# A feed-forward network in two passes of seven block products each

## The reference

```python
mod = silu(c) @ W_mod + b_mod
sh_msa, sc_msa, g_msa, sh_mlp, sc_mlp, g_mlp = split(mod, 6)
x = x + g_msa * attention(layernorm(x) * (1 + sc_msa) + sh_msa)
x = x + g_mlp * (gelu((layernorm(x) * (1 + sc_mlp) + sh_mlp) @ W1 + b1) @ W2 + b2)
```

## Time and profile before

| | |
|---|---|
| median of 3 runs | 2998.91 us (2998.82 to 3001.7) |
| the profiled execution's own time | 2999.62 us |
| its span, first to last instruction | 2997.8 us |
| mean granted clock of TensorE | 0.997 of full speed |

### The profile page before, as it was taken

How to read it: one execution, slowest core, us unless ns; L and a number is a source line. 1 busy time by engine, 2 the same in 40 slices (tenths; PEclk the granted TensorE clock), 3 DMA queues, 4 the chain that set the end, 5 groups by cost and what they waited for, 6 DMA issues and landing times.

```text
span 2997.8 us, 63187 instructions
## 1 busy us (share of the span) xinstructions
PE 2961.3 (99%) x25634; PEld 2419.0 (81%) x25634; DVE 1986.8 (66%) x2891; ACT 1390.0 (46%) x2875; POOL 787.1 (26%) x513
## 2 busy tenths in 40 slices
PE   8999999999998999999999999999999999999998
PEld 5999889999886777777777777777888888888887
DVE  4589886565535888888888888887565433343432
ACT  2366654323213777777777777776223211211111
POOL 1011110000001444444444444445553110111110
PEclk9999999999999999999999999999999999999999
DMA  5643326563595333333333333332672010010100
GB/s 184 221 160 112 113 90 249 215 228 99 187 320 172 109 94 86 86 86 93 93 87 93 89 100 90 86 86 78 249 258 92 29 36 1 29 36 29 36 15 15
DMA packets 223352, 339.35 MB, mean 113 GB/s; under 512 B 29096, under 2 KB 142920, under 8 KB 218728
## 3 DMA queue, kind: packets, MB, share of 16 engines
q1 hardware_dynamic: 214212, 329.08, 34.3%
q0 software_dynamic: 576, 6.29, 0.6%
q10 hardware_dynamic: 8292, 0.05, 0.2%
HBM read 211.15 MB, written 124.20 MB: 112 GB/s over the span
## 4 chain that ended last, share of the span: by engine, by line
PE 65%; DMA 1%; DVE 1%; ACT 0%; issue 0%; POOL 0%; SPq 0%; DVEq 0%; ACTq 0%; POOLq 0%
PE b_po L1787 16%; PE b_ps L1758 12%; PE d_pf L2261 12%; PE d_po L2272 12%; PE b_tp_act L1770 7%; PE c_po L2034 3%; PE b_tp_dve L1770 3%; DMA c_ot<-o_t 1%; DVE c_ol L2050 0%; PE d_pt L2253 0%; DVE o_first_rest L2050 0%; ACT b_p L1726 0%; POOL d_y L2202 0%; DVE norm_st L1082 0%; DVE x_second_rest L2057 0%
## 5 line engine op out<-in xcount | busy, mean ns | idle before, releaser
L1817 DVE TENSOR_REDUCE b_nm<-b_ps 128x1 f32<-128x1024 f32 x512 | 602.0, 1217 | 17.8 <-PE b_ps L1758 4.5
L1726 ACT ACTIVATE b_p<-b_ps,b_nm 128x1024 f32<-128x1024 f32 x512 | 564.6, 1112 | 8.9 <-DVE b_nm L1817 8.9
L1787 PE MATMUL b_po<-b_pt,b_v 128*64 128x256 f32 x4096 | 498.4, 385 | 0.8 <-DVE b_pt L1837 0.8
L1731 ACT ACTIVATE b_pt<-b_tp_act 128x512 f32<-128x512 f32 x512 | 307.9, 601 | 305.6 <-PE b_tp_dve L1770 305.6
L1837 DVE COPY b_pt<-b_tp_dve 128x512 f32<-128x512 f32 x512 | 351.4, 686 | 117.6 <-PE b_tp_dve L1770 117.5
L1770 PEld LDWEIGHTS b_tp_act<-ident,b_p 64*128 64x128 f32 x4096 | 311.7, 138 | 116.9 <-issue 100.6
L1787 PEld LDWEIGHTS b_po<-b_pt,b_v 128*64 128x64 f32 x4096 | 272.1, 136 | 128.4 <-ACT b_pt L1731 0.9
L2236 ACT ACTIVATE d_ge<-d_pf,b_t 128x512 f32<-128x512 f32 x128 | 88.2, 689 | 575.6 <-PE d_pf L2261 575.6
L1770 PE MATMUL b_tp_act<-ident,b_p 64*128 64x64 f32 x4096 | 347.6, 225 | 2.4 <-issue 2.4
L1770 PE MATMUL b_tp_dve<-ident,b_p 64*128 64x64 f32 x4096 | 348.2, 225 | 0.0
L2327 DVE CAST d_gh<-d_ge 128x512 fp32r<-128x512 f32 x128 | 64.6, 505 | 404.0 <-ACT d_ge L2236 403.8
(11 more groups left out here) (344 smaller groups left out, 6428.9 us busy)
## 6 DMA issues: line engine op xcount, KB each, us to landing
b_raw_q<-q_t SPq DMA_DIRECT2D x124, 256.0 KB, 4.2
k_t<-p_out SPq DMA_DIRECT2D x64, 256.0 KB, 2.2
q_t<-p_out SPq DMA_DIRECT2D x64, 256.0 KB, 2.3
v_n<-p_out SPq DMA_DIRECT2D x64, 256.0 KB, 3.6
b_v<-v_n SPq DMA_DIRECT2D x32, 512.0 KB, 3.9
b_raw_k<-k_t SPq DMA_DIRECT2D x124, 128.0 KB, 4.3
c_ot<-o_t SPq DMA_DIRECT2D x7, 2048.0 KB, 10.5
a_x<-x SPq DMA_DIRECT2D x32, 256.0 KB, 3.1
```

Of the source, the lines that this page charges most:

```text
L1726: act.activation(pr[k % 4][:], ps[k % 2][:], ACT.Exp, bias=nm[:, k % 4:k % 4 + 1], accum_out=rs[:, n:n + 1]).then_inc(exp_done, 1)
L1731: act.activation(dst, src, ACT.Copy).then_inc(t_out[0], 1)
L1787: mm = pe.matmul(po[rows, (blk % 2) * 2 * P:(blk % 2 + 1) * 2 * P], vt[u][:, kc, rows], pt[blk % 2][h][:, kc, :], start=(kc == 0), stop=(k ...
L1817: dve.tensor_reduce(nm[:, k % 4:k % 4 + 1], ps[k % 2][:], axis=AX.X, op=ALU.max, negate=True).then_inc(max_done, 1)
```

## The change

The feed-forward network becomes two passes, each with seven block products.

- Pass 1 (`hidden`) goes over 32 tiles v = 4g + p: group g of 512 rows and piece p of W1. A tile's seven products (12 matmuls of 256 columns each) land in five banks. ScalarE copies the first, VectorE makes five sums, ScalarE does the Gelu of four blocks in halves of 256 columns, and GpSimd makes four sums of the Gelu blocks, which are the operand sums of pass 2. The seven blocks, 256 KB each, are written to a tensor in HBM, `hidden_blocks`. A tile's seven places in SBUF are one of two sets; a set is free when its stores have landed (`free`). Stores are issued in two parts, `store_kept` (three blocks) and `store_sums` (four).
- Pass 2 (`back`) reads the 224 blocks back one by one through a ring of 14 places, 7 of them ahead. Each is split (`high_r` on ScalarE, `rest_r` on VectorE) and used in 12 matmuls of 256 columns. Seven banks accumulate over the four pieces, and `drained` empties them after each group: three plain sums, then four gated ones, each with a multiplication in place, and GpSimd's four additions.
- Four pieces of W1 are loaded, summed and split: two in `output_projection`, two within pass 1's first group. W2's four pieces take the same places: the first three are loaded as pass 1's last tiles free them, the last at its end. The first seven blocks of pass 2 are loaded and split within pass 1's last group.
- TensorE waits for the operand parts product by product (`NEEDED`), no longer once for a whole operand.
- Row statistics for the second group move into the last group of `output_projection`.

The core of the diff (the loops that set the order; the rest renames places and semaphores):

```diff
...
-    cols = t["w_qkv"].rearrange("(k p) n -> p k n", p=P)
+def load_w(queue, t, o, p, loaded, name="w_qkv"):
+    cols = t[name].rearrange("(k p) n -> p k n", p=P)
...
-                        for n in (2 * g - 2, 2 * g - 1):
-                            sp.dma_start(w1_part(w1_raw, n), w1_part(t["w1"].rearrange("(k p) n -> p k n", p=P), n)).then_inc(w1_in, 16)
+                    if g == 1:
+                        load_w(sp, t, w[0], 0, w1_in, "w1")
                 else:
+                    sp.wait_ge(m_done, g * GT)
+                    sp.wait_ge(w1_in, 32)
+                    load_w(sp, t, w[1], 1, w1_in, "w1")
+                    sp.wait_ge(o_split, g * KO)
+                    sp.wait_ge(y_out[0], 16 * B)
+                    sp.wait_ge(y_out[1], 16)
+                    sp.dma_start(y1[:], y2[512:1024, :].rearrange("(a p) f -> p a f", p=P)).then_inc(y1_in, 16)
                     for n in range(GT):
+                        if n == GT - 1:
+                            sp.wait_ge(m_done, NG * GT)
+                            sp.wait_ge(w1_in, 64)
+                            load_w(sp, t, w[2], 2, w1_in, "w1")
                         sp.wait_ge(y_done, g * GT + n + 1)
                         sp.dma_start(y2[(g * GT + n) * P:(g * GT + n + 1) * P, :], yt[hf][:, n, :]).then_inc(y_out[hf], 16)
+                    sp.wait_ge(w1_in, 96)
+                    load_w(sp, t, w[3], 3, w1_in, "w1")
...
+                if g in (3, NG - 1):
+                    p = g // 4
+                    act.wait_ge(w_sums, 4 * p + 4)
+                    for m in range(4):
+                        act.copy(flat(high(w[p], *GROUPS[m])), flat(raw(w[p], *GROUPS[m]))).then_inc(w_high, 1)
...
+                if r in (11, 28):
+                    p = r // 28
+                    dve.wait_ge(w1_in, 32 * p + 32)
+                    for n in range(4):
+                        block_sum(dve, w[p], SUMS_W, n, w_sums, 4 * p)
...
+                if r in (30, 31):
+                    rest_w(1, 2 * (r - 30))
+                    rest_w(1, 2 * (r - 30) + 1)
...
+    ORDER = (0, 5, 4, 6, 1, 2, 3)
+    RING, LEAD = 14, 7
+    TURNS = (0, 2, 1, 3)
...
+        PRODUCTS = ((0, 0, p_a, True), (5, 5, p_b, True), (4, 3, p_d, True), (6, 4, p_e, True),
+                    (1, 1, p_a, False), (2, 2, p_f, True), (3, 6, p_e, False))
...
+        def free(engine, v, kind):
+            if v >= 2:
+                engine.wait_ge(out_done[v % 2][kind], 32 * (v // 2))
...
+            def store_kept(v):
+                sp.wait_ge(gelu_done, 4 * v + 4)
+                for first, last in ((0, 2), (3, 4)):
+                    sp.dma_start(gq[v][:, first:last, :], places[v % 2][:, first:last, :]).then_inc(out_done[v % 2][0], 16)
...
+                v, i = block_of(n)
+                if n % 28 == 0:
+                    for u in range(2):
+                        for kind in range(2):
+                            sp.wait_ge(out_done[u][kind], 32 * 2 * (n // 28 + 1))
+                if n >= RING:
+                    sp.wait_ge(n_done, n - RING + 1)
+                if n >= 4:
+                    sp.wait_ge(r_in[n % 4], 16 * (n // 4))
+                o, r = ring_place(n)
+                sp.dma_start(flat(raw(o, r)), gq[v][:, i, :]).then_inc(r_in[n % 4], 16)
...
+                if v == NV - NP:
+                    sp.wait_ge(m_done, 7 * (NV - NP))
+                    for n in range(LEAD):
+                        load_block(n)
+                if g == NG - 1:
+                    if p == NP - 1:
+                        sp.wait_ge(m_done, 7 * NV)
+                        for n in range(LEAD, LEAD + 4):
+                            load_block(n)
+                    load_w2(p)
+                store_kept(v)
+                store_sums(v)
+                if v == NV - NP:
+                    sp.wait_ge(z_done, GT * NG)
+                    load_rows(0)
+            for n in range(LEAD + 4, RING):
+                load_block(n)
...
+            for v in range(NV):
+                g, p = divmod(v, NP)
+                if p == 0 and 1 <= g < NG - 1:
+                    rstds(g + 1)
+                u = places[v % 2]
+                for n, (o, a, b, op) in enumerate(SUMS_W):
+                    if n == 0:
+                        pool.wait_ge(gelu_done, 4 * v + 3)
+                    else:
+                        pool.wait_ge(s_sums, 4 * v + n)
+                    if n == 2:
+                        pool.wait_ge(gelu_done, 4 * v + 4)
+                    pool.tensor_tensor(u[:, o, :], u[:, a, :], u[:, b, :], op).then_inc(s_sums, 1)
...
+                    cols = slice(i * 256, (i + 1) * 256)
+                    a = act.activation(places[v % 2][:, place, cols], src[:, cols], ACT.Gelu, bias=b1[:, j + i:j + i + 1])
...
+                act.wait_ge(m_done, 7 * v + 1)
+                free(act, v, 1)
+                act.copy(u[:, 4, :], p_a[:]).then_inc(copies, 1)
+                if v:
+                    act.wait_ge(sums, 5 * v)
+                    gelu(v - 1, 1, places[(v - 1) % 2][:, 1, :])
+                if v == 1:
+                    act.wait_ge(prev.y_done, B * BT)
+                    for m in range(4):
+                        high_w(2, m)
+                if v == 2:
...
+                if more and p == 3:
+                    for m in range(0 if g == 0 else 2, 4):
+                        high_x(g + 1, m)
+                if more and p == 1:
...
+                if v >= NV - 2:
+                    for m in range(4):
+                        high_w(NP + v - NV + 2, m)
+                act.wait_ge(m_done, 7 * v + 5)
+                free(act, v, 0)
+                gelu(v, 0, p_a)
+                act.wait_ge(sums, 5 * v + 3)
+                gelu(v, 3, u[:, 3, :])
+                if more and p == 1:
+                    modulate(g + 1, 2)
+                    modulate(g + 1, 3)
+                if more and p == 2 and g:
+                    high_x(g + 1, 0)
+                    high_x(g + 1, 1)
+                act.wait_ge(sums, 5 * v + 4)
+                gelu(v, 2, u[:, 2, :])
+            act.wait_ge(sums, 5 * NV)
+            gelu(NV - 1, 1, places[(NV - 1) % 2][:, 1, :])
+            for n in range(LEAD, NB + LEAD):
+                if n in (LEAD, LEAD + 8):
+                    for m in range(4):
+                        high_w(NP + 2 + (n - LEAD) // 8, m)
...
+            def bank_free(v, step):
+                if step == 0 and v:
+                    pe.wait_ge(gelu_done, 4 * v - 3)
+                if step == 1 and v:
+                    pe.wait_ge(sums, 5 * v - 4)
+                if step == 2 and v:
+                    pe.wait_ge(sums, 5 * v - 3)
+                if step == 3 and v:
+                    pe.wait_ge(sums, 5 * v)
+                if step == 4:
+                    pe.wait_ge(copies, v + 1)
+                if step == 5 and v:
+                    pe.wait_ge(sums, 5 * v - 1)
+                if step == 6:
+                    pe.wait_ge(sums, 5 * v + 3)
...
+                    pe.wait_ge(x_rest, 4)
+                for step, (wi, xi, out_, start) in enumerate(PRODUCTS):
+                    bank_free(v, step)
+                    if p == 0 and g and step in NEEDED:
+                        pe.wait_ge(x_rest, 4 * g + NEEDED[step])
+                    if g == 0 and step in (0, 1, 3):
+                        pe.wait_ge(w_rest, 4 * p + (1, 3, 3, 4)[step])
+                    if v == 0 and step == 5:
+                        pe.wait_ge(prev.gated_done, B * BT)
+                    hidden(g, p, wi, xi, out_, start)
+                    if g + 1 < NG and p == 1 and step in (1, 2, 4, 5):
+                        transposes(g + 1, (1, 2, 4, 5).index(step))
+            for n in range(NB):
+                v, i = divmod(n, 7)
+                g, p = divmod(v, NP)
+                if g == 0 and i in NEEDED:
+                    pe.wait_ge(w_rest, 4 * (NP + p) + NEEDED[i])
...
+                if g and p == 0:
+                    if i == 0:
+                        pe.wait_ge(d_copies, g)
+                    pe.wait_ge(d_sums, 7 * (g - 1) + (0, 1, 2, 4, 5, 6, 7)[i])
+                pe.wait_ge(r_rest, n + 1)
...
+                        dve.wait_ge(w1_in, 96)
+                        for n in range(3):
+                            w_sum(2, n)
+                    if at_ == (0, 3):
+                        w_sum(2, 3)
+                    if at_ == (0, 4):
+                        dve.wait_ge(w1_in, 128)
+                        for n in range(3):
+                            w_sum(3, n)
+                    if at_ == (1, 0):
+                        w_sum(3, 3)
+                    if at_ == (1, 1):
+                        rest_w(2, 0)
+                    if at_ == (1, 2):
+                        normed(1, 2)
+                        rest_w(2, 1)
+                    if at_ == (1, 3):
+                        normed(1, 3)
+                    if at_ == (1, 4):
+                        rest_w(2, 2)
```

(58 more changed lines are left out.)

668 lines of the change are left out of this document (378 added, 290 removed).

## The result

The changed kernel takes 2982.21 us (2979.05 to 2983.45, 4 runs) against 3000.03 (2998.82 to 3001.7, 4 runs) before: a ratio of 0.9938, 95% interval 0.9925 to 0.995. That is 18 us less where 46 were forecast, and 0.2 us outside the range. Its profiled execution took 2979.05 us, 25 more than the forecast's sum of 2954.0.

What follows compares the result with a forecast made beforehand. TensorE, busy 99% of the span, was taken as the bound. Terms: 2999.62 - 60.6 + 7 + 4 + 4 = 2954.0 us by the profiled execution, 2953 by the median; range 2941 to 2982, chance 0.8.

Steps and rivals of the forecast that it cites:

- first group, stalls: Pass 1's first group: TensorE waits for normalisations while two W1 pieces are still made; +7 us (4 to 11).
- groups 1 to 6, stalls: Pass 1's groups 1 to 6: late third sums and ScalarE's copy waiting for stores; +4 us (0 to 25).
- last group, stalls: Pass 1's last group: no term of its own; DMA called hidden at 1.8 MB of blocks a tile, 175 GB/s.
- handover (pieces 1 to 4): From pass 1 to pass 2: waits for W2's late pieces and ScalarE's casts; +4 us (2 to 7).
- pass 2 afterwards: Rest of pass 2: VectorE's draining falls 3 to 6 us behind, covered by a lead of 8.6 us; 0 us.
- The matmuls: Feed-forward stage: 5376 narrow matmuls for 3072, 119.7 ns each; 657.8 us against 718.4, 60.6 us less.
- the rival of dear narrow matmuls: Feed-forward matmuls of 256 columns at 171 ns instead of 119.7: stage 933 us, kernel 3213 us; chance 0.01.
- One of the prediction's own signs: Pass 1: the prediction is wrong if tiles take above 11 us after the first group.
- The factor 1.4 for VectorE beside GpSimd: Pass 1: block sums and subtractions beside GpSimd cost 1 to 1.8 times their price; 1.4 taken.
- The second rival: VectorE beside GpSimd as second bound: 20 to 40 us instead of 15, 2960 to 2980, at 2972; chance 0.25.
- The places' loop: Pass 1's copy awaits stores from two tiles before: 8.9 us a turn, under 10.5; as bounding rival 3034 us, chance 0.05.
- The end: After the last product: sum, multiplication, GpSimd's last addition and two stores, 7.4 us against 8.1; 0 us with the start.

Runs made afterwards that it cites:

- e6: Changed kernel with GpSimd's four additions of each tile covering 32 of 512 columns, order and waits kept; 25.2 us faster by the medians.
- e16: Changed kernel with GpSimd's additions cut to 32 of 512 columns, each behind a 4-column power that keeps the chain long; 2967.24 us.
- e3: Changed kernel with loads of blocks 0 to 6 ahead of tile 27's stores and the end's first rows loaded in pass 2; last group 3.8 us shorter.
- e14: e12 with VectorE's third and fourth addition of the tile before moved from behind the second to behind the fourth sum; 3026.11 us.
- e12: Changed kernel with e11's move, casts spread, block loads before tile 27's stores, two normalisations earlier, end loads one by one; groups 1 to 6 259.4 us.
- e15: Changed kernel with only the additions of tiles 0 to 30 moved to VectorE, at e14's later places; 3047.55 us.
- e11: Changed kernel with additions of tiles 0 to 30 on VectorE, behind the next tile's first and second sums; groups 1 to 6 from 257.8 to 260.7 us.
- e10: e6 plus four 512-column GpSimd additions per tile on a tile nothing waits for, after the stores are released; 2962.97 us.
- e7: Changed kernel with TensorE waiting for all four operand parts before a group's or piece's first product; 13.3 us slower by the medians.

## Why the prediction was off

Terms up to the last matmul; the bare time is 41.8 us a group with transposes (e6: 250.6/6), and 40.2 a group without or four pieces (336 x 119.7 ns).

```
                                forecast   measured
pass 1, bare                       336.0      332.6
pass 2, bare                       321.8      321.8
first group, stalls                  7.0        9.9
groups 1 to 6, stalls                4.0        7.2
last group, stalls                   0         13.4
handover (pieces 1 to 4)             4.0       11.0
pass 2 afterwards                    0          0.5
sum                                672.8      696.4
```

- **The matmuls** were right: 120 ns, full clock wherever TensorE isn't stopped. This is the whole gain, and the rival of dear narrow matmuls is out. Pass 1's term was 3.4 us too high.
- **The last group** is the step that failed, with 13.4 of the 23.6 us missed. The forecast's sum has no term for it: I called DMA hidden by the 1.8 MB of a tile's blocks alone, and took for its VectorE the load of the steady groups. In each of its last three tiles four W2 operand sums and two or three subtractions of blocks stand beside the five sums, in the last two four subtractions of W2's parts as well. e16 and e6 show 6.6 us for the contention and 3.6 for the chain, which leaves 3.2. e3's 3.8 us for the order on SP lie within these and are not to be added. One of the prediction's own signs came here: tiles above 11 us after the first group (13.4 in the mean; 10.7 in groups 1 to 6).
- **The handover** was mis-sized, 11.0 for 4 (2 to 7). Its mechanism, ScalarE's casts waiting for W2's sums ahead of the blocks' casts, held: spreading them gives 4.0. What I left out is the 2 MB burst at block 20, which shows once that stall is gone, and the clock.
- **First group and groups 1 to 6** were mis-sized by 2.9 and 3.2, inside their ranges. The factor 1.4 for VectorE beside GpSimd was close for subtractions (1608/1219 = 1.32); the normalisations, which I left at their own price, were the ones that doubled, and TensorE waits for just those (8.1 us).
- **The clock** was in no term: 9.0 us, spread over the rows above. Stalls were priced as if only their own length counted.
- **The second rival**, at 2972, named the cause best: e6 puts its price at 25 us, of which the additions' place in the chain is a part. I gave it 0.25. Its sizes were not right: subtractions at 1.32 and not 1.8 times their price, additions at 1.43 us and not 2.28, 7.2 us and not 18 in groups 1 to 6, and it had no term for the last group either. That 2972 lies nearer to the measured time than 2953 is in part luck.
- **The places' loop** was rightly judged near its bound and not on it.
- **The end** took 2.1 us more, not none: a gate multiplication beside GpSimd took 1.26 to 1.36 instead of 0.69 us, three times over. The start gave back 0.8.

The Trainium skill (SBUF — State Buffer, "Who interferes with whom") was used for its rule on two SBUF inputs. What it says of one input holds only outside VectorE's two-port modes, a condition that the prediction left out; it also says that `tensor_scalar` can run in such a mode and then contends. That d_z doubles, while the statistics (679 and 678 ns) and the sums with a PSUM operand (688 and 690) do not change, agrees with it; whether d_z runs in that mode no run here shows.

## What to carry to other kernels

When a stage gets shorter, work out each engine's load again for its first and last group, where extra loads and operand making stand, and not for the steady part alone. A stall of TensorE is priced with what follows it: here 29 us of waits came with 9 us lost at the lower clock. An addition on a "free" engine has two prices, the traffic it puts beside its neighbour and the chain it stands in; before moving it, find both the operation that it would delay and the buffer that it would release later: here the early place took back in one stretch what it gave in others, and the place three products later cost 62 to 67 us (e14 against e12, e15 against e11).

## What the runs showed of the hardware that I had not expected

- GpSimd doubled a VectorE operation with a single SBUF tile as input: d_z took 1020 ns in the mean (up to 1517) beside additions, 541 without them. The trace before had shown it once: of four such normalisations (c_z), the first ran beside a GpSimd addition and took 1516 ns, the others 534.

```profile
L2084 DVE TENSOR_SCALAR c_z<-c_y,norm_mv,norm_rstd x4: 534/534/1516, 2135.0 to 2137.3; 128x512 f32<-128x512 f32 x4
```

- It is not GpSimd being busy that does it: powers of 4 columns, 1.02 us each and as much GpSimd time, left VectorE's normalisations and subtractions at 541 and 1219 ns. Nor does the amount of its traffic alone decide: e10's met other operations, and d_z took 650 ns.
- The granted clock fell to 0.50 behind or within TensorE's waits in the midst of a stage at 1.00: 20.5 us in all in the changed kernel, none in this stage before. With whole waits (e7) it was 34.1 us, with TensorE busy for 29.7 of them, which costs 15.
